# A six-layer float32 encoder: who makes the low parts of its weights, where in the queues, and how its biases are read

## The reference, cut to what matters

```python
# encoder, 6 layers: x is 2048 tokens of 256, d_ff = 1024, 16 heads of 16
for l in range(6):
    q, k, v = x @ Wq[l] + bq[l], x @ Wk[l] + bk[l], x @ Wv[l] + bv[l]
    a = causal_linear_attn(elu(q) + 1, elu(k) + 1, v)     # chunks of 128 tokens
    x = layer_norm(x + a @ Wo[l] + bo[l], g1[l], be1[l])
    x = layer_norm(x + gelu(x @ W1[l] + b1[l]) @ W2[l] + b2[l], g2[l], be2[l])
```

## Time and profile before

| | us |
|---|---|
| median of 3 runs | 1565.05 (1564.83 to 1565.6) |
| the profiled execution | 1564.37 |
| its span, first to last instruction | 1562.6 |
| TensorE (PE) busy | 1466.7 |
| VectorE (DVE) busy | 1261.3 |
| GpSimd (POOL) busy | 1023.3 |
| ScalarE (ACT) busy | 981.3 |

### The profile page before, as it was taken

The page is one execution under the profiler, slowest core; times in us unless marked ns, Lnnn a source line. Parts: engine busy times, 40 slices in busy tenths (PEclk is TensorE's granted clock), DMA queues, the critical chain, the costliest instruction groups (busy, mean ns, idle before and its releaser), DMA issues. The chain is left out here.

```text
span 1562.6 us, 38554 instructions
## 1 busy us (share of the span) xinstructions
PE 1466.7 (94%) x15926; PEld 1162.4 (74%) x15926; DVE 1261.3 (81%) x2103; ACT 981.3 (63%) x1604; POOL 1023.3 (65%) x941
## 2 busy tenths in 40 slices
PE   4699999999999999999999999999999899899898
PEld 3578888888888888888888888888887565565434
DVE  4779888888888898888988888888884899898556
ACT  4466666756666665676666676666644678787445
POOL 5265777757677666775667766677568588866634
PEclk8899999999999999999999999999999899999999
DMA  6120001200111001110011100110205344443001
GB/s 136 39 68 19 19 23 35 64 25 19 25 37 61 25 19 25 40 58 24 19 25 52 50 20 19 25 42 12 41 4 154 126 161 156 141 150 98 1 1 54
DMA packets 103871, 82.53 MB, mean 53 GB/s; under 512 B 28816, under 2 KB 91920, under 8 KB 103696
## 3 DMA queue, kind: packets, MB, share of 16 engines
q1 hardware_dynamic: 103696, 80.06, 18.3%
HBM read 50.79 MB, written 14.68 MB: 42 GB/s over the span
## 5 line engine op out<-in xcount | busy, mean ns | idle before, releaser
L737 POOL TENSOR_TENSOR e_h_lo<-e_h_f,e_h_hi 128x512 fp32r<-128x512 f32 x192 | 262.8, 1377 | 198.1 <-ACT e_h_hi L553 195.7
L552 ACT ACTIVATE e_h_f<-e_pr,e_h_bias 128x512 f32<-128x512 f32 x192 | 131.9, 687 | 226.1 <-PE e_pr L177 220.7
L844 DVE TENSOR_TENSOR e_am<-e_sc,c_amask 128x1024 f32<-128x1024 f32 x192 | 225.7, 1216 | 52.2 <-PE e_sc L407 52.2
L1810 DVE TENSOR_REDUCE x_mx<-x_psS 128x4 f32<-128x1024 f32 x128 | 154.4, 1208 | 32.4 <-PE x_psS L1414 32.3
L175 PE MATMUL e_tr<-e_W_hi,e_h_hi 128*128 128x256 f32 x576 | 165.4, 287 | 9.6 <-DVE X L801 9.2
L175 PE MATMUL e_pr<-e_yT_hi,e_W_hi 128*128 128x512 f32 x384 | 167.5, 436 | 2.2 <-ACT e_h_hi L553 2.2
L176 PE MATMUL e_tr<-e_W_lo,e_h_hi 128*128 128x256 f32 x576 | 162.8, 283 | 0.0
L177 PE MATMUL e_tr<-e_W_hi,e_h_lo 128*128 128x256 f32 x576 | 162.8, 283 | 0.0
L1582 ACT ACTIVATE x_ex<-x_psT 128x1024 f32<-128x1024 f32 x128 | 130.9, 1023 | 49.6 <-PE x_psT L1436 48.1
L176 PE MATMUL e_pr<-e_yT_lo,e_W_hi 128*128 128x512 f32 x384 | 151.9, 396 | 0.0
L177 PE MATMUL e_pr<-e_yT_hi,e_W_lo 128*128 128x512 f32 x384 | 151.7, 395 | 0.0
(11 more groups left out here) (286 smaller groups left out, 4428.8 us busy)
## 6 DMA issues: line engine op xcount, KB each, us to landing
e_raw_m<-in_L_attn_W_dram SPq DMA_DIRECT2D x12, 1024.0 KB, 5.4
x_qs<-query_rows SPq DMA_DIRECT2D x48, 256.0 KB
e_x_raw<-e_x_blocks SPq DMA_DIRECT2D x368, 32.0 KB, 1.9
x_ks<-key_rows SPq DMA_DIRECT2D x48, 128.0 KB, 2.7
query_rows<-x_q_hi SPq DMA_DIRECT2D x16, 256.0 KB, 2.2
query_rows<-x_q_lo SPq DMA_DIRECT2D x16, 256.0 KB, 2.4
x_ctok<-in_ctx_dram SPq DMA_DIRECT2D x8, 256.0 KB, 3.0
x_xo<-in_x_dram SPq DMA_DIRECT2D x8, 256.0 KB, 2.9
```

Source lines behind the costliest of these rows:

```text
L552: act.activation(h_f[:, m % HR, :], ps_pr[m % 2][:, :], ACT.Gelu, bias=h_bias[:, m:m + 1])
L737: pool.tensor_tensor(h_lo[:, m, :], h_f[:, m % HR, :], h_hi[:, m, :].bitcast(F32), ALU.subtract).then_inc(h_lo_done, 1)
L844: dve.tensor_tensor(am[:, s % 2, c, :, :, :], ps_sc[:, :, c * 2 * P:(c + 1) * 2 * P].rearrange("p r (h n) -> p r h n", n=P), amask[:, :].u ...
L1810: dve.tensor_reduce(mx[:, N % 2, :, 0:HG].rearrange("p i (a h) -> p h a i", a=2)[:, pair], ps_s[pair][:, :, :].rearrange("p a (i j) -> p a ...
```

## The change

- Low part of W1, layers 1 to 5: GpSimd makes the first two of the four pieces, VectorE the other two, between `phi(1)` and `phi(2)` of q = 0 (`w1_lo_part`, with a semaphore `w1_lo_rest` of its own, on which TensorE and SP wait too). So GpSimd's `rsqrt(1)` at q = 0 has two ops ahead of it instead of four. In layer 0 GpSimd makes all four.
- High part of W2: ScalarE makes all four pieces ahead of gelu(0), not behind gelu(2) and gelu(3).
- Low part of W2: four pieces ahead of h_lo(2), h_lo(4), h_lo(6) and behind h_lo(7), not two pairs ahead of h_lo(3) and h_lo(4).
- Biases: ScalarE and VectorE read their column of a table of all layers. The copy at q = 0 and the two ops at q = 2 go; the two ops at the start work on 24 columns instead of 4.

```diff
@@ SP, load_w2 (both places)
                     sp.wait_ge(w1_lo, l + 1)
+                    sp.wait_ge(w1_lo_rest, l + 1)
                     load_w2(l)
@@ TensorE, mlp_up
                         pe.wait_ge(w1_lo, l + 1)
+                        pe.wait_ge(w1_lo_rest, l + 1)
@@ ScalarE
-                    if j == 0 and (q < 0 or q == NT - 1):
-                        act.wait_ge(qk_bias_set, 2 * (t // NT + 1))
-                    act.activation(qkT[:, j, :], qk_bank(j), ACT.Relu, bias=qk_bias[:, j:j + 1], scale=-1.0).then_inc(qk_min, 1)
+                    if j == 0 and q < 0:
+                        act.wait_ge(qk_bias_set, 2)
+                    col = t // NT * 2 * KC + j
+                    act.activation(qkT[:, j, :], qk_bank(j), ACT.Relu, bias=qk_bias[:, col:col + 1], scale=-1.0).then_inc(qk_min, 1)
...
-                    if q == 0:
-                        act.wait_ge(h_bias_set, l + 1)
                     if u == final:
                         cross.values(0, cross.early(0))
+                    if q == 0:
+                        act.wait_ge(raw_2_loaded, 16 * (l + 1))
+                        wait(act, m_full, SB * NT * l)
+                        w_m("W2", w2_hi, 0)
+                        w_m("W2", w2_hi, 1)
                     gelu(0)
                     gelu(1)
...
-                    if s in (0, 1) and q == 0:
-                        if s == 0:
-                            act.wait_ge(raw_2_loaded, 16 * (l + 1))
-                            wait(act, m_full, SB * NT * l)
-                        w_m("W2", w2_hi, s)
@@ GpSimd
+            W2_LO = (2, 4, 6)
+
+            def w2_piece(layer, j):
...
+                cols = slice(j * TT, (j + 1) * TT)
+                if j % 2 == 0:
+                    pool.wait_ge(w2_hi, 2 * layer + j // 2 + 1)
+                a = pool.tensor_tensor(flat_lo[:, cols], raw_m[:, cols], flat_hi[:, cols], ALU.subtract)
+                if j == 3:
+                    a.then_inc(w2_lo, 1)
...
                 if q == 0 and l > 0:
                     w_m("W1", w1_hi, l, w1_lo, 0)
-                    w_m("W1", w1_hi, l, w1_lo, 1)
...
-                        if m in (3, 4) and q == 0:
-                            w_m("W2", w2_hi, l, w2_lo, m - 3)
+                        if m in W2_LO and q == 0:
+                            w2_piece(l, W2_LO.index(m))
...
+                    for j in range(len(W2_LO), 4 if q == 0 else 0):
+                        w2_piece(l, j)
@@ VectorE
+                def w1_lo_part(layer):
...
+                    dve.wait_ge(w1_hi, 2 * layer + 2)
+                    for j in (2, 3):
+                        cols = slice(j * TT, (j + 1) * TT)
+                        a = dve.tensor_tensor(flat_lo[:, cols], raw_m[:, cols], flat_hi[:, cols], ALU.subtract)
+                    a.then_inc(w1_lo_rest, 1)
...
                 if attn:
-                    for j in range(2 * KC):
+                    for j in range(KC):
                         phi(j)
-                if q == 0:
-                    dve.wait_ge(rest_loaded, 16 * (1 + FC + KC))
-                    wait(dve, gelu_done, FC * u)
-                    set_bias(h_bias, h_bias_all, FC, l, h_bias_set)
+                if q == 0 and l > 0:
+                    w1_lo_part(l)
+                if attn:
+                    for j in range(KC, 2 * KC):
+                        phi(j)
...
-                if more and q == NT - 2:
-
-                    dve.wait_ge(phi_done, 4 * t + 4)
-                    dve.tensor_scalar(qk_bias[:, :], qk_bias_all[:, bass.ds((l + 1) * 2 * KC, 2 * KC)], -1.0, None,
-                                      ALU.mult).then_inc(qk_bias_set, 1)
-                    dve.tensor_scalar(qk_bias1[:, :], qk_bias_all[:, bass.ds((l + 1) * 2 * KC, 2 * KC)], 1.0, None,
-                                      ALU.add).then_inc(qk_bias_set, 1)
```

More of the change, by code:

```diff
@@ L99, in encoder @@
     aT, a_nrm = qkT[:, KC:2 * KC, :], ktok[:, :, :, :].rearrange("p b c n -> p b (c n)")
-    qk_bias_all, qk_bias, qk_bias1 = sb_att("qk_bias_all", [L * 2 * KC]), sb_att("qk_bias", [2 * KC]), sb_att("qk_bias1", [2 * KC])
+    qk_bias_all, qk_bias, qk_bias1 = sb_att("qk_bias_all", [L * 2 * KC]), sb_att("qk_bias", [L * 2 * KC]), sb_att("qk_bias1", [L * 2 * KC])
     x_raw = sb_att("x_raw", [KC, TT])
@@ L108, in encoder @@
     be1_columns = sb("be1_columns", [L * KC])
-    h_bias_all, h_bias = sb("h_bias_all", [L * FC]), sb("h_bias", [FC])
+    h_bias = sb("h_bias", [L * FC])
     yT_hi, yT_lo = sb("yT_hi", [KC, TT], F32R), sb("yT_lo", [KC, TT], F32R)
@@ L157, in encoder @@
     ln_done = {i: sem(f"ln{i}_done") for i in (1, 2)}
-    qk_bias_set, h_bias_set = sem("qk_bias_set"), sem("h_bias_set")
+    qk_bias_set = sem("qk_bias_set")
     attn_set = sem("attn_set")
@@ L164, in encoder @@
     qkv_lo, o_lo, w1_lo, w2_lo = sem("qkv_lo"), sem("o_lo"), sem("w1_lo"), sem("w2_lo")
+    w1_lo_rest = sem("w1_lo_rest")
     def steps(step):
@@ L220, in _ @@
                 for c in range(FC):
-                    sp.dma_start(h_bias_all[:, c::FC], dram["b1"][:, blk(c)].rearrange("l p -> p l")).then_inc(rest_loaded, 16)
+                    sp.dma_start(h_bias[:, c::FC], dram["b1"][:, blk(c)].rearrange("l p -> p l")).then_inc(rest_loaded, 16)
                 for c in range(KC):
@@ L250, in step @@
                     sp.wait_ge(w1_lo, 1)
+                    sp.wait_ge(w1_lo_rest, 1)
                     load_w2(0)
@@ L551, in gelu @@
                         act.wait_ge(h_lo_done, FC * u + m - HR + 1)
-                    act.activation(h_f[:, m % HR, :], ps_pr[m % 2][:, :], ACT.Gelu, bias=h_bias[:, m:m + 1])
-                    act.activation(h_hi[:, m, :], ps_pr[m % 2][:, :], ACT.Gelu, bias=h_bias[:, m:m + 1]).then_inc(gelu_done, 1)
+                    act.activation(h_f[:, m % HR, :], ps_pr[m % 2][:, :], ACT.Gelu, bias=h_bias[:, l * FC + m:l * FC + m + 1])
+                    act.activation(h_hi[:, m, :], ps_pr[m % 2][:, :], ACT.Gelu, bias=h_bias[:, l * FC + m:l * FC + m + 1]).then_inc(gelu_done, 1)
                 def head_pair_hi(c):
@@ L670, in w_m @@
                     a = pool.tensor_tensor(flat_lo[:, cols], raw_m[:, cols], flat_hi[:, cols], ALU.subtract)
-                if part == 1:
-                    a.then_inc(done, 1)
+                a.then_inc(done, 1)
+            W2_LO = (2, 4, 6)
+            def w2_piece(layer, j):
+                flat_hi = hi["W2"][:, :, :].rearrange("p c n -> p (c n)").bitcast(F32)
+                flat_lo = lo["W2"][:, :, :].rearrange("p c n -> p (c n)")
+                cols = slice(j * TT, (j + 1) * TT)
[4 more added lines that the diff above has]
+                    a.then_inc(w2_lo, 1)
             w_qkv(1)
@@ L718, in step @@
                     w_m("W1", w1_hi, l, w1_lo, 0)
-                    w_m("W1", w1_hi, l, w1_lo, 1)
+                    w_m("W1", w1_hi, l, w1_lo_rest, 1)
                 if more and q == NT - 2:
@@ L776, in _ @@
             cross = nxt.vector(dve)
-            def set_bias(out, every, n, l, done):
-                dve.tensor_copy(out[:, :], every[:, bass.ds(l * n, n)]).then_inc(done, 1)
             for half_kv in range(2):
@@ L790, in _ @@
             dve.wait_ge(biases_loaded, 16 * 2 * KC)
-            dve.tensor_scalar(qk_bias[:, :], qk_bias_all[:, 0:2 * KC], -1.0, None, ALU.mult).then_inc(qk_bias_set, 1)
-            dve.tensor_scalar(qk_bias1[:, :], qk_bias_all[:, 0:2 * KC], 1.0, None, ALU.add).then_inc(qk_bias_set, 1)
+            dve.tensor_scalar(qk_bias[:, :], qk_bias_all[:, :], -1.0, None, ALU.mult).then_inc(qk_bias_set, 1)
+            dve.tensor_scalar(qk_bias1[:, :], qk_bias_all[:, :], 1.0, None, ALU.add).then_inc(qk_bias_set, 1)
             def residual(i, s, n, tile, ready, added):
@@ L834, in step @@
                 more = l < L - 1
+                def w1_lo_part(layer):
+                    flat_hi = hi["W1"][:, :, :].rearrange("p c n -> p (c n)").bitcast(F32)
+                    flat_lo = lo["W1"][:, :, :].rearrange("p c n -> p (c n)")
+                    dve.wait_ge(w1_hi, 2 * layer + 2)
[3 more added lines that the diff above has]
+                    a.then_inc(w1_lo_rest, 1)
                 def low(out, bank, part):
@@ L884, in phi @@
                     dve.wait_ge(qk_exp, 4 * t + j + 1)
-                    dve.scalar_tensor_tensor(qkT[:, j, :], qk_bank(j), qk_bias1[:, j:j + 1], qkT[:, j, :],
+                    col = t // NT * 2 * KC + j
+                    dve.scalar_tensor_tensor(qkT[:, j, :], qk_bank(j), qk_bias1[:, col:col + 1], qkT[:, j, :],
                                              ALU.add, ALU.max).then_inc(phi_done, 1)
```

## The result

The changed kernel takes 1552.45 us (median of 4, 1551.2 to 1553.49) against 1565.32 for the kernel before; the ratio is 0.9915, with a 95% interval of 0.990 to 0.993. The prediction was 1553, range 1542 to 1559. The profiled execution took 1551.2 us, its span is 1549.5.

What follows compares the result with a forecast made beforehand. VectorE being late for TensorE, together with what holds it up, was taken as the bound; 5 x 1.3 + 5 x 0 + 5 x 0.92 + 0.8 = 11.9 us off gave 1553 us, range 1542 to 1559.

Steps and rivals of the forecast that it cites:

- The bound, and the two excesses: Encoder: VectorE is late for TensorE, 3.87 us over the floor in q = 0 windows, 0.92 in q = 2, five each.
- Part 1: W1 split, q = 0: rsqrt about 1.9 us after the Wk matmul, VectorE's W1 ops about 1.6 and 3.0 us.
- Rival A: VectorE's W1 ops are not stretched by GpSimd; 2.84 us a layer gained, 1545 us; chance 20%.
- the first gate: In q = 0, TensorE's wait for VectorE's residual (2,2), which frees the bank of the second yT transpose; now 0.4 us.
- Part 2: No bias copy in q = 0: residual (2,2) ends at 266.05 instead of 267.36, gain 1.3 us, bounds 0 and 2.84.
- The sum 5 x 1.3: The gain from q = 0 of layers 1 to 5, 1.3 us each, within the 11.9 us expected in all.
- Part 3: W2's high-part copies ahead of gelu(0) run 271.0 to 273.2 in ScalarE's idle time, hidden by 0.3 us.
- Rival D: Slower by ScalarE's queue: W2 copies and gelu(0) wait for load_w2, a landing of 17 us; 1568 us; chance 4%.
- Part 4: W2's low part in four places: last attn_lo still meets h_lo(7), 0.6 us wait stays; gain 0, bounds 0 and 1.03.
- the wait at Wo: TensorE's 0.6 us wait in q = 0 for VectorE's last attn_lo, forecast to stay at 0.6 to 0.9 us.
- Part 6: Step 0: TensorE's 1.3 us wait for a gelu behind stretched W2 ops eases; gain 0.8 us, between 0.3 and 1.3.
- The sum: Total gain of 11.9 us over q = 0, q = 2 and step 0, giving a median of 1553 us; chance 55%.

Runs made afterwards that it cites:

- e7: The kernel before, with two buffers padded or moved so that all others lie at the changed kernel's addresses, no instruction different: 1565.74 us for 1566.14, ratio 0.9995.
- e4: The changed kernel with VectorE's two W1 ops moved ahead of phi(0): 1545.23 us, ratio 0.9866 to the kernel before.
- e1: The kernel before with the bias tables alone: 1556.58 us, ratio 0.9936 to the kernel before.
- e2: The kernel before with the W1 split alone, two pieces on VectorE and two on GpSimd: 1558.77 us, ratio 0.995.
- e5: The changed kernel with W2's low pieces at m = 2, 3, 4 and the last behind VectorE's last attn_lo: 1547.49 us, ratio 0.9872.
- e3: The changed kernel with both parts of W2 at their old places: 1553.93 us, ratio 0.9919 to the kernel before.

## Why the prediction was right, point by point

- **The bound, and the two excesses.** Right. q = 2 lost 0.83 us a window on average for 0.92 expected. The waits went entirely; the missing 0.08 is the new floor, which I had not foreseen and which e7 puts down to addresses.
- **Part 1, turns.** Right to 0.1 us: from issue to end 1.65 and 2.89 us for 1.6 and 3.0; rsqrt 1.87 us after the Wk matmul for 1.9. e4 shows the cause, since the same ops were only moved, and with that got another GpSimd op beside them. Rival A, that the ops run free, is refuted for this place, and its price was about right: where they do run free (e4, at another place), the first gate is gone and the kernel is at 1545.
- **Part 2, the gate.** Mechanism right, size off. Residual (2,2) ended 16.75 us after the Wk matmul, where my sum gave 17.04 and the kernel before 18.35, so the gain was 1.6 us and not 1.3. Phi(3) ended 0.13 us sooner than I had it, and k_lo began 0.2 us sooner. TensorE's wait at the yT transpose was therefore 0.9 us and not over 1, and the window 48.7 us, with 0.3 of the difference to 49.3 from part 4. The sum 5 x 1.3 was the largest error, some 1.5 us too small. What I didn't see is that either half of it would have given most (e1 and e2).
- **Part 3, W2's high part.** Right. The copies run 2.20 us from 268.81, released by the down matmul and not by the DMA, and gelu(0) idles 0.24 us behind them, for 0.3:

```profile
268.81 2.20 ACT L506 ACTIVATE e_W_hi<-e_raw_m 128x512 fp32r<-128x512 f32 x4 [0.73 <-PE e_pr L178]
271.25 0.69 ACT L557 ACTIVATE e_h_f<-e_pr,e_h_bias 128x512 f32<-128x512 f32 x1 [0.24 <-PE e_pr L178]
```

  Rival D had therefore nothing to work on.
- **Part 4, W2's low part.** I expected no gain because the last attn_lo would meet another h_lo. It did (1.45 us), and e5 shows that this alone kept the wait at Wo. But parts 3 and 4 together gained 0.31 us a window in place of 0 (e3 against the changed kernel). 0.2 of it is the wait for a gelu that went, which the forecast did not look at; whether the high or the low part's move did that is not shown.
- **Part 6, step 0.** 0.56 us for 0.8.
- **The sum.** 11.9 us expected, 12.9 measured by the medians and 13.1 by the spans. The q = 0 windows gave 9.2 us for 6.5 (parts 2 to 4, the clock's share left out), q = 2 gave 4.15 for 4.6, step 0 gave 0.56 for 0.8. The late op of u = 11, which I had not foreseen, and the luck of the clock in u = 12 added 1.7 us; the slower floor, and the start and end, took 2.5. So the median is closer to the forecast than the terms deserve.

## What to carry to other kernels

Where two engines take turns, as VectorE and GpSimd do here, the cost of an instruction depends on what the other engine runs at that moment: put short two-input ops beside the other engine's short ones, not beside its longest, and ask for the op on the critical path when the other is idle. Look at a moved op's new neighbours before its length. And judge two cures of one late gate together: 1.3 and 1.4 us alone were 1.6 in company, while cures of two gates added up.

## What the runs showed of the hardware

- VectorE's subtraction of two 128x512 float32 tensors in SBUF took 0.68 us beside a 128x4 op of GpSimd (e4) and up to 2.90 us beside GpSimd's 128x1024 multiplication. It stretched GpSimd's ops too: the 128x1024 addition behind it took 2.88 us for 2.4. In these rows the two take turns per instruction. VectorE's ops on 4 or 8 columns of SBUF can be held in the same way (in the kernel before 1.03 and 1.80 us, where they take 0.16 to 0.17 otherwise); the 128x256 residual op with one input in PSUM was not (0.38 to 0.43 us, all 192 of them).
- The pace of TensorE depends a little on where buffers lie in SBUF: 46.75 or 46.83 us for a step of 550 matmuls with no wait, with nothing but addresses changed (e7). Which buffer does it was not looked for, so this stays open.
